# Second norm turned on VectorE, and the masked product moved behind the last scores

## The reference

```python
out = layernorm(x, g1, b1)
out = out @ (sf_w * mask).T + sf_b        # the masked product
x1 = x + out
out = layernorm(x1, g2, b2)               # the second norm
out = attention(out)                      # relu scores, causal, divided by their sum; 16 heads of 16
x2 = x1 + out
out = layernorm(x2, g3, b3)
out = relu(out @ ff1_w.T + ff1_b) @ ff2_w.T + ff2_b
x = layernorm(x + x2 + out)               # the fourth norm, without gain
# then, for every token: argmax over 8 centroids picks an expert,
# h = relu(layernorm(x) @ w1[e].T + b1[e]) @ w2[e].T + b2[e], mixed by a sigmoid, and a last layernorm
```

## Time and profile before

| | us |
|---|---|
| median of 3 runs (lowest, highest) | 829.07 (827.1, 830.39) |
| the profiled execution | 829.01 |
| its span, first to last instruction | 827.2 |
| TensorE busy, share of the span | 807.6, 98% |
| VectorE | 543.3, 66% |
| ScalarE | 343.5, 42% |
| GpSimd | 282.9, 34% |

### The profile page before, as it was taken

How to read it: one execution, slowest core, us unless ns; L and a number is a source line. 1 busy time by engine, 2 the same in 40 slices (tenths; PEclk the granted TensorE clock), 3 DMA queues, 4 the chain that set the end, 5 groups by cost and what they waited for, 6 DMA issues and landing times.

```text
span 827.2 us, 19008 instructions
## 1 busy us (share of the span) xinstructions
PE 807.6 (98%) x7090; PEld 546.5 (66%) x7090; DVE 543.3 (66%) x1536; ACT 343.5 (42%) x573; POOL 282.9 (34%) x395
## 2 busy tenths in 40 slices
PE   9999999999999999999999999999999999999994
PEld 6654475476466467558557646869989977777673
DVE  6665368767767857876788765524678556666572
ACT  2444415414523531640641452333323366667660
POOL 4505011431512403313233051325454454533432
PEclk9999999999999999999999999999999999999998
DMA  7800020130030020031011034223643898988940
GB/s 272 253 2 27 11 68 1 53 78 0 27 103 1 27 53 1 2 75 55 1 52 53 8 107 132 103 94 132 220 155 108 314 310 296 333 283 317 325 195 17
DMA packets 63953, 96.42 MB, mean 117 GB/s; under 512 B 39347, under 2 KB 52276, under 8 KB 55926
## 3 DMA queue, kind: packets, MB, share of 16 engines
q1 hardware_dynamic: 58566, 83.56, 30.2%
q0 software_dynamic: 4864, 11.10, 4.2%
q10 hardware_dynamic: 432, 0.54, 0.2%
HBM read 84.22 MB, written 11.23 MB: 115 GB/s over the span
## 4 chain that ended last, share of the span: by engine, by line
PE 93%; DVE 3%; issue 1%; ACT 1%; another core or an unknown queue 0%; POOL 0%; DVEq 0%; POOLq 0%; ACTq 0%
PE ps L678 14%; PE ps L672 14%; PE ps L780 10%; PE ps L799 10%; PE ps L611 9%; PE ps L635 8%; PE ps L816 4%; PE ps L832 4%; PE ps L584 4%; PE ps L488 3%; PE ps L643 3%; PE ps L538 2%; PE ps L530 2%; PE ps L766 1%; PE ps L498 1%
## 5 line engine op out<-in xcount | busy, mean ns | idle before, releaser
L678 PE MATMUL ps<-ff2T,hT 128*128 128x256 f32 x512 | 121.6, 385 | 0.2 <-ACT hT L1683 0.2
L672 PE MATMUL ps<-x3x,ff1T 128*128 128x512 f32 x256 | 118.2, 605 | 0.1
L678 PEld LDWEIGHTS ps<-ff2T,hT 128*128 128x128 f32 x512 | 94.3, 190 | 21.0 <-issue 8.1
L1691 ACT ACTIVATE arena<-ps 128x1536 f32<-128x1536 f32 (+3 forms) x49 | 65.1, 1329 | 102.3 <-DVE arena L1118 101.7
L799 PE MATMUL ps<-w_sb,arena 128*128 x400 | 95.6, 382 | 0.1
L1908 POOL TENSOR_TENSOR rs_ln<-mv_ln,eps 128x4 f32<-128x4 f32 x23 | 4.7, 206 | 258.7 <-DVE mv_ln L965 258.7
L672 PEld LDWEIGHTS ps<-x3x,ff1T 128*128 128x128 f32 x256 | 46.0, 189 | 59.0 <-issue 50.9
L799 PEld LDWEIGHTS ps<-w_sb,arena 128*128 128x128 f32 x400 | 72.2, 190 | 12.2 <-issue 4.3
L1118 DVE SCALAR_TENSOR_TENSOR arena<-ps,arena 128x512 f32<-128x512 f32 (+4 forms) x59 | 45.1, 771 | 52.6 <-PE ps L635 34.1
L611 PE MATMUL ps<-arena 32*128 32x512 f32 (+7 forms) x896 | 73.0, 434 | 1.8 <-ACT hT L1137 1.4
L1683 ACT ACTIVATE hT<-ps,col 128x512 f32<-128x512 f32 x64 | 43.2, 684 | 51.2 <-PE ps L672 51.2
(11 more groups left out here) (244 smaller groups left out, 1533.5 us busy)
## 6 DMA issues: line engine op xcount, KB each, us to landing
arena<-in_w SPq DMA_DIRECT2D x27, 1024.0 KB
hT<-in_w SPq DMA_DIRECT2D x16, 1024.0 KB
wts<-in_w SPq DMA_DIRECT2D x9, 1024.0 KB
w_sb<-in_w SPq DMA_DIRECT2D x8, 1024.0 KB, 5.4
token_store<-x SPq DMA_DIRECT2D x8, 520.0 KB, 3.6
...
```

Of the source, the lines that this page charges most:

```text
L672: last = eng.matmul(ps[:, 6 + m % 2, :], ff1T[:, kd, m * P:(m + 1) * P], xT3[:, kd, :], start=kd == 0, stop=kd == KD - 1)
L678: last = eng.matmul(quarter(6, t), hT[:, m, t * P:(t + 1) * P], ff2T[:, m, :], start=m == 0, stop=m == FM - 1)
L1691: eng.activation(o, i, ACT.Relu).then_inc(s_sa, 1)
```

## The change

For the six seams b = 1 to 6:

- The masked product of b + 1 stands on TensorE right behind the last scores, before the last two weighings, in banks 7 and 6 and no longer in 2 and 3. VectorE adds it before it turns the weighed values.
- The second norm's normalisation goes from VectorE to GpSimd (`pool_ln2`), ahead of the scatters. VectorE turns the rows in 16 block transposes behind the context (`dve_turn_rows2`). ScalarE applies gain and bias in place (`act_gain2`). The eight TensorE transposes and the evictions of banks 0 and 1 are gone.
- The second layer's output of batches 0 to 5 lies in other banks: tile 0 in bank 6, tiles 1 and 2 in score bank 0, tile 3 in bank 7. VectorE adds it in three pieces, `ADDED`: tile 0 behind the statistics of step 7, tiles 1 and 2 behind the residual add of the attention, tile 3 in step 1 of the next batch. `added(f)` counts these adds. Batches 6 and 7 keep the old banks and two pieces.
- Waits follow: the second half of the masked product waits for the add of tile 0, the first scores for that of tiles 1 and 2, the output in bank 0 for the end of the last scores' ReLU.

All six seams read alike in order; the rows here are those of batch 2. In them `wts` holds the masked weights, `w_sb` the turned input, `hT` the hidden layer, `ctxT` lies in `arena` as scores' weights and `x1` do, `x3x` is the attention's residual sum or the third norm's turned rows, `r2xhT` the second residual, the normalised rows or the second norm's turned rows, `st_ln` and `mv_ln` the norms' statistics and means. TensorE before, from the scores of step 8 (L611) to the half tile ahead of the queries:

The diff, cut to its core:

```diff
+N_APART = NB - 2
+ADDED, ADDED_LAST = ((0, 1), (1, 3), (3, 4)), ((0, 2), (2, 4))
...
+        def added(f):
+            return len(ADDED) * min(f, N_APART) + len(ADDED_LAST) * max(0, f - N_APART)
+        def output(f, t):
+            return ((6, 0), (0, 0), (0, 1), (7, 0))[t] if f < N_APART else (6 + t // 2, t % 2)
...
-        def pe_sf(eng, b, tiles=range(NT), bank=2):
+        def pe_sf(eng, b, tiles=range(NT), banks=(2, 2)):
             if b == 0:
...
                     eng.wait_ge(s_xTe, t // 2 + 1)
+                if b > 1 and t == 2:
+                    eng.wait_ge(s_r3, added(b - 2) + 1)
                 for kd in range(KD):
-                    last = eng.matmul(quarter(bank, t), src[:, kd, t * P:(t + 1) * P], sfT[:, kd, :], start=kd == 0,
+                    last = eng.matmul(quarter(banks[t // 2], t), src[:, kd, t * P:(t + 1) * P], sfT[:, kd, :], start=kd == 0,
                                       stop=kd == KD - 1)
...
         def pe_queries_keys(eng, b):
-            eng.wait_ge(s_x1, 2 * b + 2)
-            for kd, ready in ((0, s_Te["ln2"]), (1, s_Td["ln2"])):
-                eng.wait_ge(ready, b + 1)
+            eng.wait_ge(s_sa, STEPS * b)
+            for kd in range(KD):
+                eng.wait_ge(s_Te["ln2"], 2 * b - 1 + kd)
                 for m in range(KD):
...
                         last.then_inc(s_q, 1)
-            if b:
-                eng.wait_ge(s_x2, 2 * b)
+            eng.wait_ge(s_x2, 2 * b)
             for m in range(KD):
...
                 eng.wait_ge(s_ke, 2 * b + 1)
+                if b:
+                    eng.wait_ge(s_r3, added(b - 2) + 2)
             else:
...
             if b:
-                eng.wait_ge(s_r3, 2 * b)
+                eng.wait_ge(s_r3, added(b))
             else:
...
-                eng.wait_ge(s_r3, 2 * b - 1 + m)
+                if b - 1 >= N_APART:
+                    eng.wait_ge(s_r3, added(b - 1) + 1 + m)
+                elif m:
+                    eng.wait_ge(s_r3, added(b))
+                else:
+                    eng.wait_ge(s_x1, 2 * b + 4)
             if 0 < b < NB - 1 and m == 6:
...
         def pe_ffn2_part(eng, b, t, part):
+            bank, half = output(b, t)
             for m in part:
-                last = eng.matmul(quarter(6, t), hT[:, m, t * P:(t + 1) * P], ff2T[:, m, :], start=m == 0,
+                last = eng.matmul(quarter(bank, half), hT[:, m, t * P:(t + 1) * P], ff2T[:, m, :], start=m == 0,
                                   stop=m == FM - 1)
-            if t % 2 and FM - 1 in part:
+            if t + 1 in [hi for _, hi in (ADDED if b < N_APART else ADDED_LAST)] and FM - 1 in part:
                 last.then_inc(s_f2, 1)
...
                     pe_affinity(eng, g, 6)
-                for k in (UNITS1 if b == 1 else UNITS)[n]:
-                    pe_unit(eng, f, k)
+                if n == STEPS - 1 and more:
+                    pe_sf(eng, b + 1, banks=(7, 5))
+                else:
+                    for k in (UNITS1 if b == 1 else UNITS)[n]:
+                        pe_unit(eng, f, k)
                 if n == 5 and g >= 0:
...
             elif more:
-                pe_sf(eng, b + 1)
-                pe_units(eng, f, NT - 2, 0)
+                eng.wait_ge(s_sa, STEPS * (b + 1))
+                pe_units(eng, f, 1, 0)
+                pe_units(eng, f, 1, 1)
+                pe_units(eng, f, 2, 0)
                 pe_proj_o(eng, b)
-                pe_units(eng, f, NT - 2, 1)
-                pe_ln2_T(eng, b + 1)
+                pe_units(eng, f, 2, 1)
                 pe_units(eng, f, NT - 1, 0)
...
-                eng.wait_ge(s_r3, 2 * f + 1)
+                eng.wait_ge(s_r3, added(f) + 1)
                 slot_pe_x_T(eng, 0)
...
-        def dve_add_sf(eng, b, parts=range(2), bank=2):
+        def dve_add_sf(eng, b, parts=range(2), banks=(6, 6)):
             eng.wait_ge(s_pa, b)
             eng.wait_ge(s_rs["ln1"], b + 2)
             for i in parts:
-                dve_add_half(eng, b, i, bank)
+                dve_add_half(eng, b, i, banks[i])
                 dve_half_var(eng, b, i)
         def dve_ln2(eng, b):
-            if b == 2:
-                eng.wait_ge(s_T["ln3"], 2)
             for i in range(2):
...
         def dve_ln3(eng, b):
-            if b < NB - 1:
-                eng.wait_ge(s_T["ln2"], 2 * b + 4)
+            if b == 0:
+                eng.wait_ge(s_T["ln2"], 4)
             dve_normalise(eng, b, "ln3", x2, xh)
...
+        def dve_turn_rows2(eng, b):
+            eng.wait_ge(s_x2h, 2 * (b - 1))
+            dve_turn_blocks(eng, xT, xh, range(N_TURN)).then_inc(s_Td["ln2"], 1)
...
         def dve_add_ffn(eng, b, i):
-            eng.wait_ge(s_f2, 2 * b + i + 1)
+            first, end = (ADDED if b < N_APART else ADDED_LAST)[i]
+            eng.wait_ge(s_f2, added(b) + i + 1)
             eng.wait_ge(s_r2, b + 1)
-            v = r2[:, 2 * i:2 * i + 2, :]
-            eng.tensor_tensor(v, halves(6 + i), v, ALU.add).then_inc(s_r3, 1)
-            eng.wait_ge(s_r3, 2 * b + i + 1)
-            return dve_row_stats(eng, "ln4", r2, i)
+            v = r2[:, first:end, :]
+            bank, half = output(b, first)
+            eng.tensor_tensor(v, halves(bank)[:, half:half + end - first, :], v, ALU.add).then_inc(s_r3, 1)
+            eng.wait_ge(s_r3, added(b) + i + 1)
+            for t in range(first, end):
+                last = eng.bn_stats(stats["ln4"][:, t, :], r2[:, t, :])
+            return last
...
                     dve_turn_rows3(eng, f, TURN3[2])
-                    dve_mean_var(eng, "ln4", dve_add_ffn(eng, g, 1))
+                    dve_mean_var(eng, "ln4", dve_add_ffn(eng, g, 2))
                 if b > 1 and n == 2:
...
                     dve_ln1_stats(eng, b + 1)
-                if n == 8 and b:
+                    dve_add_ffn(eng, f, 0)
+                if n == 8 and not more:
                     dve_add_ffn(eng, f, 0)
...
                         slot_dve_in_norm(eng, 1)
+            if more and b:
+                dve_add_sf(eng, b + 1, banks=(7, 5))
             dve_turn_out(eng, b, 2)
...
             if more and b:
-                dve_add_sf(eng, b + 1)
-                dve_ln2(eng, b + 1)
-                dve_ln2_T(eng, b + 1)
+                dve_turn_rows2(eng, b + 1)
             dve_mean_var(eng, "ln3", dve_add_o(eng, b))
+            if more and b:
+                dve_add_ffn(eng, f, 1)
             if not more:
...
+        def act_gain2(eng, b):
+            eng.wait_ge(s_Td["ln2"], b + 1)
+            for kd in range(KD):
+                eng.activation(xT[:, kd, :], xT[:, kd, :], ACT.Identity, bias=col[:, C_B2 + kd:C_B2 + kd + 1],
+                               scale=col[:, C_G2 + kd:C_G2 + kd + 1]).then_inc(s_Te["ln2"], 1)
...
             if more and b:
-                act_ln2_T(eng, b + 1)
+                act_gain2(eng, b + 1)
...
+        def pool_ln2(eng, b):
+            eng.wait_ge(s_T["ln3"], 2)
+            eng.wait_ge(s_av, AVS * (b - 1) + released(5))
+            for i in range(2):
+                pool_rstd_half(eng, b, i, "ln2")
+                eng.wait_ge(s_rs["ln2"], 2 * b + i + 1)
+                for t in (2 * i, 2 * i + 1):
+                    last = eng.tensor_scalar(xh[:, t, :], x1[:, t, :], mv["ln2"][:, t, 0:1], rstd["ln2"][:, t:t + 1],
+                                             ALU.subtract, ALU.mult)
+                last.then_inc(s_x2h, 1)
...
             eng.wait_ge(s_x, 16 * (b + 1))
-            eng.wait_ge(s_xh["ln2"], 2 * b)
+            eng.wait_ge(s_xh["ln2"], 2 * min(b, 2))
             if b > 1:
...
                 slot_pool_rstd(eng, 1, 0)
+            if more and b:
+                pool_ln2(eng, b + 1)
             if g >= 0:
...
                 pool_scatter_ids(eng, g)
-            if more:
+            if b == 0:
                 pool_rstd_ln2(eng, b + 1)
```

15 lines of the change are left out of this document (8 added, 7 removed).

## The result

| | before | changed |
|---|---|---|
| median, us (lowest, highest) | 829.36 of 4 runs (827.1, 830.39) | 837.28 of 4 runs (837.09, 837.92) |
| ratio, 95% interval | | 1.0105 (1.0093 to 1.0117) |
| profiled execution: span, us | 827.2 | 835.6 |
| TensorE busy | 807.6, 98% | 804.5, 96% |
| GpSimd busy | 282.9, 34% | 311.5, 37% |

The account below looks back on a forecast made before the run. The prediction took TensorE's gapless queue to bound the attention part. Five seams gaining 0.87 us (4.35), less 0.6 lost in batch 6, make 3.75: 829.0 - 3.75 = 825.3 us, range 822.8 to 829.0.

Parts of the forecast that it names:

- What bounds the kernel: Attention part: time is the length of TensorE's gapless queue, period 66.67 us; other engines count only when their results come late.
- the removal: Six seams: dropping the second norm's eight TensorE transposes starts queries 0.87 us earlier each, 5.2 us of queue in all.
- The move at no cost: Seams: reordering masked product and output pieces adds no TensorE time, and the ends of banks do not delay it.
- the 0.6 us in batch 6: End of batch 6: slot-table work delays mask and context, so this seam loses 0.6 us instead of gaining 0.87.
- VectorE's and ScalarE's part behind GpSimd: Before the queries: 16 VectorE block transposes take 7.1 us, then ScalarE's first half of gain and bias 0.76.
- GpSimd's normalisation, t: Each seam: one 128x256 subtract-and-multiply on GpSimd takes 0.6 us, so both halves are ready before VectorE is free.
- The slack and the break-even: Before the queries: 0.7 us slack; waits begin past t = 0.95 and equal the 0.87 gain at t = 1.17.
- Batch 6 in the break-even: Rivals' thresholds of t = 0.95 and 1.17, with all of a seam's gain eaten giving 829, applied to batch 6's seam.
- rival 2: Seams: the chain into the queries arrives late, eating part of the gain; 827 at half, 829 at all; chance 0.28.
- The seam of batch 6 with a short t: End of batch 6: projection waits 0.5 us and queries 0.9; last window 67.3 us.
- Rival 3: Seams: GpSimd's normalisation is slow, from t = 1.17, making the kernel slower; 839.5 us at t = 1.5; chance 0.10.

Follow-up runs that it names:

- experiments 1: Changed kernel with GpSimd copying the rows unnormalised in place of the second norm's normalisation in batches 2 to 7; 824.07 us, ratio 0.9939.
- experiment 2: Changed kernel with the second norm's normalisation on ScalarE, GpSimd making only the shift; 824.91 us, ratio 0.9946; measured again at 824.06 and 824.07.
- Experiment 3: Changed kernel with only masked product, banks and output pieces moved; second norm, its TensorE transposes and evictions as before; 828.33 us, ratio 0.9996.
- experiment 6: Changed kernel with another form of GpSimd's 128x256 instruction in each seam, second norm of batches 3 to 7 incomplete; 829.46 us, a single run.
- experiment 4: Changed kernel with matmuls on constants filling TensorE's wait ahead of batch 7's queries, other five seams untouched; 835.27 us, ratio 1.0076.

## Why the prediction was wrong

- **What bounds the kernel, and the removal: right.** With a short instruction the period is 66.67 less 0.87 in four windows of four (experiments 1 and 2), and the whole comes to 824.07 and 824.06 to 824.91, 0.4 to 1.2 us under the 825.3 that was forecast.
- **The move at no cost: right.** Experiment 3, but for the 0.6 us in batch 6 that the prediction had booked.
- **VectorE's and ScalarE's part behind GpSimd: right**, to 0.1 us each.
- **GpSimd's normalisation, t: the step that failed.** I had three nearby rows, a copy, a quarter of a tensor add and a power, and took the add's quarter, 0.6, "as this is plain arithmetic on one tensor". It measured 1.22. The add's quarter was a good price for a tensor form (0.61 in experiment 6), but not for a tensor-scalar form. t counts four times in a seam: 4 x 0.62 = 2.5 us. With 1.22 in it the prediction's own sum gives, as an estimate, 0.2 lost at each of five seams and 2.4 in batch 6 (halves at 448.4 + 4.9 = 453.3, queries at 461.3 against 458.84): 832.5. That is 7 of the 12 us between forecast and result; the slack, the restart and the clock below make the rest.
- **The slack and the break-even: too wide by 0.2 in t.** The wait should have begun at t = 0.95 and met the gain at 1.17. By experiment 6's waits it begins near 0.8 (1.65 / 4 = 0.41 below 1.22), and meets the gain near 0.97, where a wait of 0.55 and the restart below make 0.79. So at t = 1.22 my formula gives a loss of 0.2 a seam; it was 1.0. Of the 0.6 that the formula lacks in the wait, 0.2 is VectorE's first variance, out at 314.2 where the forecast's clock says 314.0; 0.2 is the hand-over from it to GpSimd, which begins at 314.38; 0.2 lies behind GpSimd, in turns, gain and their hand-overs (321.45 to 329.66, 8.2 for 8.0).
- **Batch 6 in the break-even: left out.** By the prediction's own rows the halves there are ready at 448.4 + 4t and VectorE is free at 451.5, so that seam loses more from t = 0.78 on, not from 0.95. At 1.17, where rival 2 says 829, it loses 2.2, and the sum is 831. The range's upper end was too low even by the prediction's own terms.
- **Restart: not in the sum.** In the stream the row of a query product takes 3.60 and begins 0.16 before the row ahead of it ends, 3.43 in the chain; behind a wait it takes 3.67 and nothing overlaps. That is 0.24 a seam: 67.68 = 66.67 - 0.87 + 1.65 + 0.24, to 0.01.
- **The seam of batch 6 with a short t: right as put** (0.37 to 0.51 for the projection, 0.82 for the queries, against 0.5 and 0.9), and worse in the changed kernel by t. What was missing is the clock: the idle time of 3.0 us cost another 1.7 (experiment 4).
- **Rival 3: right mechanism**, at 0.10 too small a chance. It had a row for it: the power takes 0.72 on two elements where the addition on two takes 0.24, so on this engine the operation can set the price at one and the same size. The range ended where this case began.

From the seams: five times 1.02 is 5.1; batch 6 costs 0.39 + 3.01 - 0.87 and 1.94 of longer query product, 4.5. That is 9.6, and the profiled span grew by 8.4. The rest comes back in the expert tiles: the changed kernel is 10.1 us behind at 616.75 and 8.3 behind at the last matmuls, with the same work on TensorE, whose busy time from 622.58 to 820.60 is 197.03 where the like stretch of before has 198.68. The seams do not seem to be the reason: from 616.75 to the last matmuls it is 203.9, before 205.7, and in the other traces 203.6 to 205.3, with 204.8, 205.0 and 205.2 in three of the kernel of experiment 2. Why it varies was not tested and stays open.
